# Graph network on one core: contiguous degree sums, and layer 1's first product woven between layer 0's sums

## The reference, cut to what matters

```python
deg = jnp.maximum(segment_sum(ones, dst), 1.0)
h = jnp.maximum(layernorm(x), 0.0)
y = h @ W_self.T + (segment_sum(h[src], dst) / deg) @ W_neigh.T + bias
x = x + layernorm(y) * gamma + beta                      # layer 0

h = jnp.maximum(layernorm(x), 0.0)
degw = segment_sum(w, dst) + 1                           # weights of the edges into a node, and a self loop
dinv = where(degw > 0, rsqrt(degw), 0)
def conv(v, W, b): return dinv * (A @ (dinv * (v @ W)) + dinv * (v @ W)) + b
y = conv(relu(conv(h, W1, b1)), W2, b2)                  # layer 1: 512 -> 256 -> 512
x = x + y / max(norm(y), 1e-12)
```

## Time and profile before

| | us |
|---|---|
| median of 3 runs | 1457.14 (1455.31 to 1458.76) |
| the profiled execution: its own time | 1453.09 |
| the profiled execution: span from first to last instruction | 1450.9 |
| PE busy in the span | 1267.2 (87%) |
| DVE busy in the span | 1015.8 (70%) |
| POOL busy in the span | 716.3 (49%) |
| ACT busy in the span | 578.1 (40%) |
| degree reductions on DVE (L1657), 20 | 45.5 |
| PE from the first layer 0 sum to the first x1 sum | 539.7 to 683.0 |

### The profile page before, as it was taken

How to read it: one execution, slowest core, us unless ns; L and a number is a source line. 1 busy time by engine, 2 the same in 40 slices (tenths; PEclk the granted TensorE clock), 3 DMA queues, 4 the chain that set the end, 5 groups by cost and what they waited for, 6 DMA issues and landing times.

```text
span 1450.9 us, 20460 instructions
## 1 busy us (share of the span) xinstructions
PE 1267.2 (87%) x4424; PEld 733.0 (51%) x4424; DVE 1015.8 (70%) x1763; ACT 578.1 (40%) x1462; POOL 716.3 (49%) x873
## 2 busy tenths in 40 slices
PE   5859899078888889877998989999999889997998
PEld 2534444033333334336876444545454568885775
DVE  8798253068888889861248268988898899888422
ACT  0211311066666640113001168888887723333210
POOL 0677777767777752766674156666666200000000
PEclk9989999589999999988999999999999999998999
DMA  8842512020000017353223367777777200002220
GB/s 335 320 140 67 196 53 74 23 102 17 19 17 24 9 46 268 103 183 98 87 88 117 109 201 229 228 225 230 220 230 217 70 1 0 1 0 84 73 91 35
DMA packets 87238, 167.89 MB, mean 116 GB/s; under 512 B 16108, under 2 KB 44654, under 8 KB 84628
## 3 DMA queue, kind: packets, MB, share of 16 engines
q1 hardware_dynamic: 59044, 102.19, 21.0%
q0 software_dynamic: 25472, 59.97, 13.8%
q10 hardware_dynamic: 2672, 5.11, 1.1%
HBM read 115.97 MB, written 51.25 MB: 115 GB/s over the span
## 4 chain that ended last, share of the span: by engine, by line
PE 45%; issue 16%; POOL 14%; DMA 11%; DVE 11%; POOLq 1%; ACT 1%; DVEq 1%; ACTq 0%
DMA arena<-p_rows,gidx 9%; POOL cell_rows L690 8%; PE pb L1092 7%; PE pb L1174 6%; PE pb L1200 6%; PE pb L1387 5%; PE pb L1358 3%; PE pb L1359 3%; PE pb L1360 3%; PE pb L1290 3%; PE pb L1208 3%; POOL tiles L744 2%; DMA cell_rows<-tiles,gidx 2%; POOL arena L744 1%; PE pb L1115 1%
## 5 line engine op out<-in xcount | busy, mean ns | idle before, releaser
L803 POOL DMA_INDIRECT arena<-p_rows,gidx x184 | 190.5, 1035 | 66.1 <-issue 60.0
L736 POOL DMA_INDIRECT dst_rows<-ering,gidx x168 | 172.4, 1026 | 100.1 <-issue 70.1
L690 POOL DMA_INDIRECT cell_rows<-tiles,gidx x168 | 168.2, 1001 | 68.0 <-issue 39.7
L1290 PE MATMUL pb<-arena 128*128 128x512 f32 x368 | 191.4, 603 | 4.2 <-ACT arena L963 4.2
L1635 DVE TENSOR_TENSOR arena<-pb,arena 128x384 f32 x272 | 150.2, 552 | 45.9 <-PE pb L1174 24.4
L1092 PE MATMUL pb<-ws,tiles 128*128 128x512 f32 (+1 forms) x360 | 146.3, 554 | 12.3 <-ACT tiles L825 12.3
L1743 DVE TENSOR_TENSOR arena<-pb,arena 128x512 f32<-128x512 f32 x184 | 124.3, 687 | 38.2 <-DMA arena<-p_rows,gidx 33.8
L1174 PE MATMUL pb<-arena 128*128 128x384 f32 x272 | 107.1, 519 | 48.1 <-POOL arena L744 45.6
L866 ACT ACTIVATE arena<-iota,free 128x128 f32<-128x128 f32 x272 | 94.3, 394 | 123.0 <-PE pb L1174 82.5
L1174 PE MATMUL pb<-tiles,arena 128*128 128x384 f32 x272 | 106.3, 514 | 22.6 <-POOL tiles L744 20.9
L1092 PEld LDWEIGHTS pb<-ws,tiles 128*128 128x128 f32 x360 | 66.7, 194 | 69.3 <-issue 53.5
(11 more groups left out here) (284 smaller groups left out, 2371.1 us busy)
## 6 DMA issues: line engine op xcount, KB each, us to landing
dst_rows<-arena SPq DMA_DIRECT2D x6, 2046.0 KB, 17.5
ering<-in_edge_attr_dram SPq DMA_DIRECT2D x41, 256.0 KB, 3.0
arena<-adj SPq DMA_DIRECT2D x10, 640.0 KB, 3.9
arena<-dst_rows SPq DMA_DIRECT2D x24, 264.0 KB, 2.8
arena<-wt_gru SPq DMA_DIRECT2D x48, 128.0 KB
ws<-dst_rows SPq DMA_DIRECT2D x22, 264.0 KB, 2.9
arena<-in_x_dram SPq DMA_DIRECT2D x18, 256.0 KB, 8.5
arena<-in_L_gnn_W_hh_dram SPq DMA_DIRECT2D x3, 1024.0 KB, 20.1
```

The source lines that it names most:

```text
L690: nc.gpsimd.indirect_dma_start(cell_rows[:, :], bass.IndirectOffsetOnAxis(gidx[:, SPAN * a + k:SPAN * a + k + 1], 0), cring[:, a, k], None ...
L736: nc.gpsimd.indirect_dma_start(dst_rows[:, :], bass.IndirectOffsetOnAxis(gidx[:, k:k + 1], 0), ering[:, k, :], None).then_inc(e_scattered[ ...
L803: nc.gpsimd.indirect_dma_start(rows[:, k, :], None, p_rows[:, :], bass.IndirectOffsetOnAxis(gidx[:, k:k + 1], 0)).then_inc(g_landed[k], 16)
L1290: nc.tensor.matmul(e_bank(k)[:], erowT[:, k % 4], w1e_sb, start=True, stop=True).then_inc(edge_mm, 1)
```

## The change

**Degrees.** `degree` now takes a group of five destination tiles, and adds the blocks of the sources s = 0 to 9 one after another with contiguous TENSOR_TENSOR additions of 5 x 128 = 640 elements: nine for a group. Matrix 0's two groups are added alternately (18 additions); matrix 1's first group stands behind layer 0's tile 0 and the second behind tile 1, each addition waiting for the one before. PE's `degrees(0)` stands behind the sums of tiles 0 and 1, no longer behind tile 3; `degrees(1)` stands behind tile 4, no longer behind 7.

**Layer 1's first product.** PE turns `h` of tile t - 3 behind layer 0's sum of tile t, and multiplies tile t - 4 behind it. ACT copies the turned tile t - 3 after it has written `h` of tile t, and scales tile t - 4 behind that. Tiles 7 to 9 are turned, and 6 to 9 multiplied, after the last sum. `dinv` is worked out after tile 4. W1 has a place of its own (in `spare`) and is loaded right behind the first two `ys` tiles; the loads of b1, W2, `w1h` and b2 are issued by ACT after the last `h`, ahead of the last three tiles' copies.

```diff
-        w1_sb = ws[:, 1].rearrange("p k f -> p (k f)")[:, 0:KT * DH].rearrange("p (k f) -> p k f", k=KT)
+        w1_sb = spare[:, 0:KT * DH].rearrange("p (k f) -> p k f", k=KT)
-        DINV_AFTER = 5
+        DINV_AFTER = 4
+        BEHIND = 3
-        act_jobs += ["deg0", "deg1"]
-        h1_jobs = [("h1T", 0)]
+        h1_jobs = ["deg0", ("h1T", 0), "deg1"]
...
@@ ACT
             load_ys(0)
             load_ys(1)
+            nc.scalar.dma_start(w1_sb, w1_1.rearrange("(k p) f -> p k f", p=P)).then_inc(w_loaded, 16)
+            def h1_turned(t):
+                if t >= 2:
+                    act.wait_ge(for_act, A[("g1", t - 2)] + 1)
+                copy_job(("h1T", t), flat(hT[:, t % 2]))
+            def g1_scaled(t):
+                act.wait_ge(for_act, A[("g1", t)] + 1)
+                if t == 0:
+                    act.wait_ge(dinv_ready, 1)
+                nc.scalar.activation(g1[:, t], act_bank(("g1", t))[:, 0:DH], ACT.Copy,
+                                     scale=dinv[:, t:t + 1]).then_inc(act_read, 1)
             for t in range(NT):
...
                 nc.scalar.activation(h[:, t], xs[:, t], ACT.Relu, bias=mv[:, t, 0:1], scale=rstd[:, t:t + 1]).then_inc(h_ready, 1)
                 if t == DINV_AFTER:
                     root("dinv", dinv[:])
+                if t >= BEHIND:
+                    h1_turned(t - BEHIND)
+                if t > BEHIND:
+                    g1_scaled(t - BEHIND - 1)
+            nc.scalar.dma_start(vec[:, 0, 0:DH], b1_1...).then_inc(vec_loaded, 16)
+            act.wait_ge(for_dve, V[("y0", NT - 1)] + 1)
+            act.wait_ge(norm_ready, NT)
+            nc.scalar.dma_start(w2_sb, w2_1...).then_inc(w2_there, 16)
+            act.wait_ge(wt_stored[0], 16 * 4)
+            nc.scalar.dma_start(ws[:, 0]..., wt_dram["w1h"]).then_inc(p_loaded, 16)
+            nc.scalar.dma_start(vec[:, 1], b2_1...).then_inc(vec_loaded, 16)
+            for t in range(NT - BEHIND, NT + 1):
+                if t < NT:
+                    h1_turned(t)
+                g1_scaled(t - 1)
@@ PE
-            sum0(2, range(NT))
-            sum0(3, range(NT))
             degrees(0)
-            for t in range(4, NT):
+            for t in range(2, NT):
                 sum0(t, range(NT))
-                if t == 7:
+                if t == DINV_AFTER:
                     degrees(1)
+                if t >= BEHIND:
+                    turn_h1(t - BEHIND)       # waits h_ready, four transposes
+                if t > BEHIND:
+                    linear_h1(t - BEHIND - 1) # waits act_read of this tile's h1T
+            for t in range(NT - BEHIND, NT + 1):
+                if t < NT:
+                    turn_h1(t)
+                linear_h1(t - 1)
@@ DVE
-            def degree(m, t):
-                return nc.vector.tensor_reduce(deg_parts[:, m, t], adj3[:, m, t * NT:(t + 1) * NT].rearrange("p s d -> p d s"),
-                                               AX_X, ALU.add)
+            def degree(m, group):
+                for s in range(1, NT):
+                    for n, part in enumerate(group):
+                        blocks_of = adj3[:, m, part.start * NT:part.stop * NT].rearrange("p (t s) d -> p t s d", s=NT)
+                        total = deg_parts[:, m, part]
+                        if s > 1:
+                            dve.wait_ge(step, chain[0] - len(group) + 1)
+                        chain[0] += 1
+                        ins = vtt(total, blocks_of[:, :, 0] if s == 1 else total, blocks_of[:, :, s], ALU.add)
+                        ins.then_inc(step, 1)
+                dve.wait_ge(step, chain[0])
...
-            for t in range(6):
-                degree(1, t)
...
-                if t < 4:
-                    ins = degree(1, 6 + t)
-                    if t == 3:
-                        ins.then_inc(deg_ready, 1)
+                if t < 2:
+                    degree(1, halves[t:t + 1])
+                    if t == 1:
+                        dve.sem_inc(deg_ready, 1)
```

More of the change, by code:

```diff
@@ L909, in _ @@
                     act.wait_ge(adj3_stored[1], 16)
-                if t == 2 * KT - 1:
+                if t == 2 * KT:
                     act.wait_ge(for_dve, V[("y0", NT - 1)] + 1)
[L912 to L915, removed]
                 nc.scalar.activation(h[:, t], xs[:, t], ACT.Relu, bias=mv[:, t, 0:1], scale=rstd[:, t:t + 1]).then_inc(h_ready, 1)
@@ L918, in _ @@
                     root("dinv", dinv[:])
[L921 to L935, removed]
+                if t >= BEHIND:
+                    h1_turned(t - BEHIND)
+                if t > BEHIND:
+                    g1_scaled(t - BEHIND - 1)
+            nc.scalar.dma_start(vec[:, 0, 0:DH], b1_1.rearrange("(a f) -> a f", a=1).to_broadcast([P, DH])).then_inc(vec_loaded, 16)
+            act.wait_ge(for_dve, V[("y0", NT - 1)] + 1)
+            act.wait_ge(norm_ready, NT)
+            nc.scalar.dma_start(w2_sb, w2_1.rearrange("(k p) f -> p k f", p=P)).then_inc(w2_there, 16)
+            act.wait_ge(wt_stored[0], 16 * 4)
+            nc.scalar.dma_start(ws[:, 0].rearrange("p k f -> p (k f)"), wt_dram["w1h"]).then_inc(p_loaded, 16)
+            nc.scalar.dma_start(vec[:, 1], b2_1.rearrange("(a f) -> a f", a=1).to_broadcast([P, D])).then_inc(vec_loaded, 16)
+            for t in range(NT - BEHIND, NT + 1):
+                if t < NT:
+                    h1_turned(t)
+                g1_scaled(t - 1)
             def turned1(t):
@@ L1227, in _, with turn_h1, linear_h1 @@
                 sum0(t, range(2 * KT, NT))
-            sum0(2, range(NT))
-            sum0(3, range(NT))
             degrees(0)
-            for t in range(4, NT):
-                sum0(t, range(NT))
-                if t == 7:
-                    degrees(1)
-            pe.wait_ge(w_loaded, 32)
-            for t in range(NT):
+            def turn_h1(t):
                 pe.wait_ge(h_ready, t + 1)
                 turn_tile(("h1T", t), h[:, t])
[L1240 to L1244, removed]
+            def linear_h1(t):
+                if t == 0:
+                    pe.wait_ge(w_loaded, 16)
+                pe.wait_ge(act_read, A[("h1T", t)] + 1)
+                linear(("g1", t), [(hT[:, t % 2], w1_sb)], DH)
+            for t in range(2, NT):
+                sum0(t, range(NT))
+                if t == DINV_AFTER:
+                    degrees(1)
+                if t >= BEHIND:
[6 more added lines that the diff above has]
+                linear_h1(t - 1)
             pe.wait_ge(act_read, A[("g1", NT - 1)] + 1)
@@ L1654, in _ @@
             dve.wait_ge(block_added, CELL_CHUNKS)
[L1656 to L1662 removed]
+            def degree(m, group):
[9 more added lines that the diff above has]
+                dve.wait_ge(step, chain[0])
+            halves = [slice(0, NT // 2), slice(NT // 2, NT)]
+            degree(0, halves)
+            dve.sem_inc(deg_ready, 1)
             dve.wait_ge(adj3_stored[0], 16)
             nc.vector.memset(xs[:, NT - 1], 0.0).then_inc(x_free, 1)
[L1665 to L1666 removed]
             dve.wait_ge(act_read, A["deg0"] + 1)
```

8 lines of the change are left out of this document (5 added, 3 removed).

## The result

| | before | after |
|---|---|---|
| median, us | 1458.21 (1455.31 to 1464.31, 11 runs) | 1464.22 (1462.50 to 1468.34, 11 runs) |
| ratio, 95% interval | | 1.0037 (1.0022 to 1.0051) |
| profiled execution, span | 1450.9 | 1465.1 |
| PE from the first layer 0 sum to the first x1 sum | 143.27 | 150.73 |
| DVE busy | 1015.8 | 998.6 |

The change makes the kernel **slower, by 5.4 us** (3.2 to 7.4: the ratio's excess times 1458.21). The forecast was 3.4 us slower.

What follows compares the result with a forecast made beforehand. PE was taken to carry the kernel from the x1 sums at 683.01; D0 + 94.8 + 17.5 put them at 686.4, 3.4 us later, so 1457.14 + 3.4 = 1460.5 us, range 1454.1 to 1464.6.

Steps and rivals of the forecast that it cites:

- D0: Start of DVE's chain of layer 0's tile 0: forecast 574.1, bounds 571.9 and 574.9, where it was 584.39.
- the hold at tile 3: Layer 0: PE's product of tile 0 waits for DVE's first four chains and both degree groups, D0 + 39.9; chance 0.62.
- clock at the restart: PE after some 20 us with almost no work restarts at the low clock: 1.6 us more.
- 10.75 per tile: Layer 0 on PE after the hold: sum 8.58, turning 0.43, product 1.73 per tile; PE sets the pace, four tiles.
- tail: From layer 0's last sum to the x1 sums: 17.5 us, between 17.0 and 17.8, where it was 42.5.
- Degree sums: DVE additions: a group of matrix 1 takes 7.74, bounds 6.2 and 7.74; matrix 0's 18 at most 15.5, hidden behind PE.
- The tiles of x: DVE's beta addition waits for x: complete at 566.4 before, delayed 2.2 (at most 3.0) by ACT's loads, to 568.6.
- the rival of no change: x lands at 566.4 as before and PE's clock is up before tile 5's sum: -0.4 us, 1456.7; chance 0.17.
- PE ahead of the hold: Layer 0: by its own work PE would be through tile 4's sum at about 590.
- Faster: Rival: tiles of x complete at 561.7 when `deg` is there, D0 567.2, -3.5 us, 1453.6; chance 0.11.
- Slower by far: Rival: POOL's scatters hold up matrix 1's 18 additions, 9.2 on the hold, +12.6 us, 1469.7; chance 0.10.

Runs made afterwards that it cites:

- w1_again: Changed kernel with W1's load issued behind `h` of tile 0, the same edit as w1_late run again; 1.0015 of the kernel before, stretch 149.48 us.
- warm: Changed kernel with PE turning tile 1 fifteen times over in its idle time ahead of the first product; stretch 149.03 us, no ratio.
- four_behind: all3 with weaving four tiles behind, tiles 6 and 7 copied between tile 9's roots, W2 and `w1h` loaded behind the last `g1`; 0.9801 of the kernel before.
- adds_early: Changed kernel with matrix 1's additions moved ahead of DVE's wait for the tiles of x; 0.9919 of the kernel before, stretch 135.56 us.
- copy_first: Changed kernel with ACT's copy of turned tile t - 3 ahead of tile t's roots and `h`; 0.9961 of the kernel before, stretch 141.57 us.
- all3: Changed kernel with the edits of adds_early, copy_first and w1_late together; 0.9873 of the kernel before, stretch 124.54 us.
- no_weave: Changed kernel with layer 1's turning and multiplying back behind layer 0's last sum, additions kept; 1.0015 of the kernel before, stretch 146.17 us.
- reductions: Changed kernel with the twenty old strided reductions in their old places instead of the additions, weaving kept; 1.0061 of the kernel before, stretch 152.96 us.
- w1_late: Changed kernel with W1's load issued behind `h` of tile 0, not behind the first two `ys` tiles; executed once, stretch 148.65 us, no ratio.

## Why the prediction was right, and where it was off

The direction and the mechanism were right, and the time lies inside the range, though the median of 1464.22 is only 0.4 below its upper end (by the ratio it is 1457.14 x 1.0037 = 1462.5). All the misses have the same sign, so none made good for another. The size was 3.4 against 5.4 by the ratio, and against 7.46 in the stretch of the two profiled executions. By terms, with 1.46 taken off the places:

| step | forecast | measured | difference |
|---|---|---|---|
| tile 0's chain starts (D0) | 574.1 | 576.17 | +2.1 |
| from D0 to the product of tile 0 (the hold at tile 3) | 39.9 | 40.28 | +0.4 |
| clock at the restart | 1.6 | 2.9 | +1.3 |
| 10.75 per tile | 43.0 for four | 43.0 | 0 |
| tail | 17.5 | 17.77 | +0.3 |
| sum against before | +3.4 | +7.46 | +4.1 |

- **Degree sums.** A group came out at 7.74 and 7.73, the upper bound. Matrix 0's 18 took 13.32 and not 15.5: there the two halves are added in turn, so that no addition waits for the one just before it (0.74 from start to start against 0.86). Hidden, as forecast.
- **The tiles of x** were the largest miss: the beta addition started at 570.64 against 568.6, and D0 lies outside its bounds. The prediction had named this as a sign that it would be wrong. The path that it stands on was right; two terms of the sum were short. The first is where x landed in the kernel before. I took 566.4, 0.9 ahead of POOL's start (no row shows this 0.9), because the edge loads were issued behind x. SP's timeline of the kernel before has them ahead of the tenth tile:

```profile
549.54 8.49 SPq L562 DMA_DIRECT2D arena<-in_x_dram  x9
558.20 0.95 SPq L536 DMA_DIRECT2D ering<-in_edge_attr_dram  x2
562.87 0.36 SPq L565 DMA_DIRECT2D arena<-in_x_dram  x1
```

So POOL's start says nothing of this tile, and busy time by window shows traffic behind 566.4:

```profile
566.00:567.00 1.00, 1.00 (x4) 0.52 (x3) 1.00 (x1) 0.00 (x0) 0.00 (x0) 1.00 0.68 198
567.00:568.00 1.00, 1.00 (x4) 0.43 (x3) 1.00 (x2) 0.00 (x0) 0.74 (x1) 1.00 0.01 4
```

The semaphore events of that trace have the last landing of x at 567.62, 1.2 later than I took it. The second term is what ACT's loads add. The last landing of x in the changed kernel is at 572.00, or 570.54 with 1.46 off: 2.9 later than before, where I had 2.2, with half of W1's load, and 3.0 as the bound. w1_again, without W1, has it 29.18 into the stretch as against 30.80, so all of W1 counts, 1.6, the full 0.5 MB at 0.35 MB per us being 1.5. The two terms make 1.9 of the 2.0. The Trainium skill, page "DMA: Bandwidth & Descriptors", section "Issuing engines are not separate DMA queues", says that the queues of all engines end in the same 16 DMA engines; the runs agree, with 1.6 us on SP's queue for 0.5 MB on ACT's.
- **The hold at tile 3** is shown by three runs that take away a part of it: 15.84 where the groups are 15.5 by moving the additions, 5.8 by moving the copy (70.90, as expected), 1.8 by moving D0 (w1_again).
- **The clock.** Both restarts that I had before me followed idling of 7 and 9.3 us, and cost 1.5 and 1.75 for one piece of work. Here both pieces paid: 1.81 on the product and 1.13 on the sum of tile 5. The term was that of one, and the upper bound had nothing for it; warm measured 2.82. That `degrees(1)`, busy for 4.43 us between two idle times, would bring the clock up (the rival of no change) is refuted: 0.50 in its window and 0.50 behind it.
- **PE ahead of the hold.** I had PE through tile 4's sum at about 590; it was there at 594.6 (596.0 with 1.46 off). Turning tile 0 waited 4.66 for its `h`, and the sum behind it ran with the clock at 0.80. The hold hides this here, and only four_behind takes it away.
- **The tail** came within 0.3, yet one wait in it was not seen: the product of tile 5 waits 1.00, because ACT's `h` of tile 8 (the row at 674.42 above) waits for the last sum, which reads `z` from the place that this `h` goes to. It hides in the wait for tile 6's copy.
- **The rivals.** "Faster" needed x before 562.5: refuted, at 570.64. "Slower by far" needed additions of more than 1 us beside POOL: the 18 of matrix 1 kept 0.86 from start to start while POOL scattered, and took the same 0.854 in adds_early, where they were all but done when POOL began (586.9 and 586.5). The Trainium skill, page "SBUF — State Buffer", section "SBUF: two separate sides", would have each side block the other. Here POOL was held up, for long once, and DVE was not:

```profile
571.65 0.97 POOL L736 DMA_INDIRECT dst_rows<-ering,gidx  x1 [0.30 <-issue]
572.92 5.51 POOL L736 DMA_INDIRECT dst_rows<-ering,gidx  x1 [0.30 <-issue]
...
603.12 1.55 POOL L736 DMA_INDIRECT dst_rows<-ering,gidx  x1 [0.88 <-issue]
```

The second of these rows lies beside the beta addition (572.10 to 577.59) and takes 5.51 where its neighbours take 0.97; the first had begun ahead of the beta addition, which took its 5.49 all the same. Beside the additions of 0.83 five scatters of nine take 1.27 to 1.55 and the others 0.97. POOL's loss is within its idling of 21.03.

**What stays open**: the gap between the stretch's 7.46 and the ratio's 5.4. In the other runs the two agree within the interval (adds_early: -7.7 in the stretch, -12.0 by the ratio; copy_first: -1.7 and -5.8; all3: -18.7 and -18.5; no_weave: +2.9 and +2.2; reductions: +9.7 and +8.9; four_behind: -27.3 and -29.0), but in w1_again the stretch is 6.2 longer than before and the ratio allows at most 5.1. Each stretch is of one execution, and the kernel before was profiled once for them; the first sums alone differed by 1.7 between w1_late and w1_again, which are the same code.

## What to carry to other kernels

Work that is woven into a loop ties the engines' queues together at the place where it stands. Before weaving, ask of each inserted instruction what stands ahead of it on its own engine, and follow that back to the slowest engine: here one copy on ACT, placed behind `h(t)` instead of ahead of it, made PE wait for DVE. Put new work on the slow engine into the waits that it has anyway, here 16.4 us of idling just ahead of 15.5 us of additions; and when the order is changed, look at the last rounds of the loop by themselves, since they keep waits that the middle hides. Count the clock on every piece of work behind a long idle time, not only on the first.

## What the runs showed of the hardware

- Behind 8.63 us of idling, twenty products of one column (4.43 us of busy PE) ran at a granted clock of 0.50, and it was still 0.50 behind them (windows 604.80 to 617.90 above). With sixty transposes in 8.53 us right behind the same twenty, it was 0.78 over their window and 1.00 after it. Without them the product paid 1.81 and the next sum 1.13.
- 0.5 MB on ACT's queue made the last tile of x on SP's queue land 1.6 us later (30.80 into the stretch as against 29.18 in w1_again): about the price of its bytes at the 0.35 MB per us that all 16 engines moved, 1.5.
- A DVE instruction with two SBUF inputs was not slowed by POOL's indirect DMAs (0.86 from start to start beside them, 0.854 without, and 5.49 for the 5120 elements in every run), while a POOL DMA that began inside the long one took 5.51 against 0.97, and ended 0.84 behind it.
- Eighteen additions of 640 elements take 13.32 when neighbours are independent and 15.38 when each takes the result of the last: 0.11 us more for each.
